# Taking the products of a graph network's last stage straight out of PSUM, with the output stage one pair of tiles later

## The reference: what is computed

```python
# layer 2 (RGCN with basis decomposition, mean aggregation, root weight and bias)
coeff = comp[edge_type]                                   # 8 coefficients for each edge
aggs = [segment_sum(x[src] * coeff[:, b:b + 1], dst) for b in range(8)]
agg = stack(aggs, axis=1) / maximum(deg, 1.0)[:, None, None]
out = concatenate([agg.reshape(N, -1), x], axis=1) @ weight.reshape(-1, 128) + bias
x = layernorm(x + out)                                    # rows without an edge get x @ root + bias only
```

## Time and profile before

| | us |
|---|---|
| median of three runs (1011.98 to 1019.42) | 1016.24 |
| the profiled execution's own time | 1006.45 |
| its span, first to last instruction | 1004.6 |
| GpSimd busy in the span | 702.8 |
| VectorE busy | 816.0 |
| TensorE busy | 827.7 |
| ScalarE busy | 649.2 |
| first gather of the last stage starts at | 698.15 |
| last scatter of the last stage starts at | 992.77 |

### The profile page before, as it was taken

The page is one execution under the profiler, slowest core; times in us unless marked ns, Lnnn a source line. Parts: engine busy times, 40 slices in busy tenths (PEclk is TensorE's granted clock), DMA queues, the critical chain, the costliest instruction groups (busy, mean ns, idle before and its releaser), DMA issues. The chain is left out here.

```text
span 1004.6 us, 19805 instructions
## 1 busy us (share of the span) xinstructions
PE 827.7 (82%) x4972; PEld 663.4 (66%) x4972; DVE 816.0 (81%) x2958; ACT 649.2 (65%) x2960; POOL 702.8 (70%) x702
## 2 busy tenths in 40 slices
PE   4789999999999999999998778774797778687882
PEld 3667777777777777777776666563675667565661
DVE  7999999999999999999997566562696867777793
ACT  3699999999999999999997567663121111121221
POOL 4277777777777777777766466566787878888784
PEclk9999999999999999999999789896799879788996
DMA  6266666666565655656563122212776556565740
GB/s 185 86 199 203 205 195 193 195 194 202 195 205 200 194 193 191 198 197 201 191 188 98 56 72 76 67 58 94 280 269 223 205 201 216 203 215 199 248 171 26
DMA packets 87719, 175.54 MB, mean 175 GB/s; under 512 B 16620, under 2 KB 33032, under 8 KB 81207
## 3 DMA queue, kind: packets, MB, share of 16 engines
q1 hardware_dynamic: 70422, 144.02, 42.2%
q0 software_dynamic: 15744, 29.71, 9.7%
q10 hardware_dynamic: 1440, 0.56, 0.2%
HBM read 105.88 MB, written 70.88 MB: 176 GB/s over the span
## 5 line engine op out<-in xcount | busy, mean ns | idle before, releaser
L648 ACT ACTIVATE junk<-ps 128x128 bf16<-128x128 f32 x884 | 235.7, 300 | 52.4 <-remote 14.2
L605 PE MATMUL ps<-work,w_cen 128*128 128x256 f32 x784 | 199.1, 411 | 14.0 <-DVE work L1029 8.6
L648 ACT ACTIVATION_READ_ACCUMULATOR junk<-ps 128x1 f32 x884 | 199.1, 232 | 0.0
L605 PEld LDWEIGHTS ps<-work,w_cen 128*128 128x128 f32 x784 | 157.7, 207 | 46.8 <-DVE work L1029 15.0
L410 POOL TENSOR_TENSOR work<-work,vec_raw 128x512 f32<-128x512 f32 x98 | 124.2, 1267 | 91.7 <-DVE work L973 90.8
L512 PE MATMUL ps<-w_cen,xT 128*128 128x128 f32 x984 | 163.3, 299 | 0.0
L512 PEld LDWEIGHTS ps<-w_cen,xT 128*128 128x128 f32 x984 | 132.7, 201 | 30.0 <-issue 30.0
L374 POOL DMA_INDIRECT x_table<-agg_all,scat_i x98 | 99.5, 1015 | 71.4 <-issue 27.0
L734 ACT ACTIVATE outb<-agg_now,st 128x128 f32<-128x128 f32 x98 | 34.0, 394 | 169.9 <-DMA out_rows<-outb,scat_i 169.5
L381 POOL DMA_INDIRECT rows<-x_table,src_i x98 | 118.4, 1208 | 31.0 <-issue 29.3
L374 POOL DMA_INDIRECT out_rows<-outb,scat_i x98 | 117.6, 1200 | 30.0 <-issue 28.5
(11 more groups left out here) (139 smaller groups left out, 1481.5 us busy)
## 6 DMA issues: line engine op xcount, KB each, us to landing
coefs<-coef_line SPq DMA_DIRECT2D x49, 1024.0 KB
rows<-in_x SPq DMA_DIRECT2D x97, 256.0 KB
x_table<-work SPq DMA_DIRECT2D x97, 256.0 KB
out_rows<-outb SPq DMA_DIRECT2D x97, 256.0 KB
x_dst_table<-x_dst SPq DMA_DIRECT2D x98, 64.0 KB
rows<-x_dst_table SPq DMA_DIRECT2D x24, 256.0 KB
rows<-in_x,src_i POOLq DMA_INDIRECT x98
same_prev<-mask_line SPq DMA_DIRECT2D x1, 1568.0 KB, 9.0
```

The lines of the kernel that those rows point to most:

```text
L605: last = pe.matmul(MT[b][:, 0:PAIR * D], w_cen[:, W_BASE + m, :], prod[:, b, m, :, :].rearrange("p t d -> p (t d)"), start=(m == 0), stop= ...
L648: last = nc.scalar.activation(junk[:, kind * CH + m, :], bank[:, cols(m, m + 1)], ACT.Square, accum_out=power[:, b, 1, TOP + kind * CH + m ...
```

## The change

In the last stage ScalarE's copy of the transposed rows goes. VectorE's two products read the rows in PSUM, in the bank where TensorE put them. Since a bank is now held until both products are made, `GX` has four banks in place of two: 4, 5, 0 and 1. TensorE waits, before it fills a bank again, for the products of four pairs before, and no longer for ScalarE. The output part of a pair moves one step later on VectorE and ScalarE (`c - 5` for `c - 4`), `OUT_LAG` from 6 to 7, and the loop has one step more. VectorE's order within a step changes: the scan now comes ahead of both products. Apart from that the SP queue issues the coefficient loads of pairs 0 to 2 in steps 120, 121 and 122 of the edge loop, in place of after its last step.

```diff
-OUT_LAG = 6
+OUT_LAG = 7
-    LAST_C = PAIRS + 3
+    LAST_C = PAIRS + 4
-        GT, GX, MT, ST = banks(4, 1), [banks(4, 1), banks(5, 1)], [banks(2, 1), banks(3, 1)], [banks(6, 1), banks(7, 1)]
+        GT, GX, MT, ST = banks(4, 1), [banks(k, 1) for k in (4, 5, 0, 1)], [banks(2, 1), banks(3, 1)], [banks(6, 1), banks(7, 1)]
...
+            def coef_load(q):
+                r = q * PAIR // (TYPE_TILES * LINE_BLOCKS)
+                sp.wait_ge(line_stored[r], 16 * len(blocks_of(r)))
+                need(sp, S["dve_prod"], 2 * (q - COEF_SLOTS + 1))
+                sp.dma_start(coefs[:, q % COEF_SLOTS, :, :, :].rearrange("p t b e -> p (t b e)"),
...
+                if 0 <= c - TYPE_STEP - 10 < COEF_SLOTS:
+                    coef_load(c - TYPE_STEP - 10)
...
-            for q in range(PAIRS):
...
+            for q in range(COEF_SLOTS, PAIRS):
+                coef_load(q)
...
             def step_c(s):                                    # TensorE
-                    need(pe, S["act_g"], s - 1)
+                    need(pe, S["dve_prod"], 2 * (s - len(GX) + 1))
...
             def step_c(s):                                    # ScalarE
-                if c < PAIRS:
-                    act.wait_ge(S["pe_g"], s + 1)
-                    need(act, S["dve_prod"], 2 * (s - 1))
-                    nc.scalar.copy(xT[:, b, 0:PAIR, :].rearrange("p c d -> p (c d)"), GX[b][:, 0:PAIR * D]) \
-                        .then_inc(S["act_g"], 1)
-                if 0 <= c - 4 < PAIRS:
-                    q = c - 4
+                if 0 <= c - 5 < PAIRS:
+                    q = c - 5
...
             def product(h):                                   # VectorE
-                            dve.wait_ge(S["act_g"], s)
+                            dve.wait_ge(S["pe_g"], s)
...
-                            xT[:, 1 - b, 0:PAIR, :].unsqueeze(1).broadcast_to([P, HALF, PAIR, D]), ALU.mult) \
+                            GX[q % len(GX)][:, 0:PAIR * D].rearrange("p (t d) -> p t d", t=PAIR).unsqueeze(1)
+                            .broadcast_to([P, HALF, PAIR, D]), ALU.mult) \
...
                 if last_pair:
-                    dve.wait_ge(S["pe_s"], s - 3)
-                    need(dve, S["act_out"], s - 5)
+                    dve.wait_ge(S["pe_s"], q + 1)
+                    need(dve, S["act_out"], q - 1)
...
-                product(0)
...
+                product(0)
+                if last_pair:
+                    own.need(at)
+                    at = variance(0, PAIR, par)
                 product(1)
```

More of the change, by code:

```diff
@@ L280, in _ @@
             sp.dma_start(w_raw[:, W_POOL, :], pool_w).then_inc(S["pool_in"], 16)
+            def coef_load(q):
[3 more added lines that the diff above has]
+                sp.dma_start(coefs[:, q % COEF_SLOTS, :, :, :].rearrange("p t b e -> p (t b e)"),
+                             coef_line[q * PAIR:(q + 1) * PAIR].rearrange("(o t) b e -> o (t b e)", o=1)
+                             .broadcast_to([P, PAIR * NB * P])).then_inc(coefs_in[q % COEF_SLOTS], 16)
             def step(s):
@@ L589, in _ @@
             pe.wait_ge(S["line_made"], LINES)
+            pe.wait_ge(S["act_a"], GROUPS)
             def step_c(s):
@@ L595, in step_c @@
                     slot = c % GATHER_SLOTS
-                    need(pe, S["act_g"], s - 1)
+                    need(pe, S["dve_prod"], 2 * (s - len(GX) + 1))
                     pe.wait_ge(x1_in[slot], 16 * PAIR * (c // GATHER_SLOTS + 1))
                     for n in range(PAIR):
-                        last = pe.transpose(GX[b][:, cols(n, n + 1)], gathered[:, slot * PAIR + n, :], ident[:, :])
+                        last = pe.transpose(GX[c % len(GX)][:, cols(n, n + 1)], gathered[:, slot * PAIR + n, :], ident[:, :])
                     last.then_inc(S["pe_g"], 1)
@@ L733, in step_c @@
                     for n in range(PAIR):
-                        last = nc.scalar.activation(out_tiles[:, q % SLOTS * PAIR + n, :], y_rows[:, b, n, :],
+                        last = nc.scalar.activation(out_tiles[:, q % SLOTS * PAIR + n, :], y_rows[:, q % 2, n, :],
                                                     ACT.Copy, scale=st[:, 7, n:n + 1])
@@ L1018, in step_c @@
                 b = c % 2
-                last_pair = 0 <= c - 4 < PAIRS
+                last_pair = 0 <= c - 5 < PAIRS
                 def product(h):
@@ L1031, in product @@
                             coefs[:, q % COEF_SLOTS, :, half, :].rearrange("p t m d -> p m t d"),
-                            xT[:, 1 - b, 0:PAIR, :].unsqueeze(1).broadcast_to([P, HALF, PAIR, D]), ALU.mult) \
+                            GX[q % len(GX)][:, 0:PAIR * D].rearrange("p (t d) -> p t d", t=PAIR).unsqueeze(1)
+                            .broadcast_to([P, HALF, PAIR, D]), ALU.mult) \
                            .then_inc(S["dve_prod"], 1)
                 if last_pair:
-                    dve.wait_ge(S["pe_s"], s - 3)
-                    need(dve, S["act_out"], s - 5)
+                    q = c - 5
+                    par = q % 2
+                    dve.wait_ge(S["pe_s"], q + 1)
+                    need(dve, S["act_out"], q - 1)
                     for n in range(PAIR):
-                        t = (s - 4) * PAIR + n
-                        last = dve.scalar_tensor_tensor(y_rows[:, b, n, :], ST[b][:, cols(n, n + 1)],
+                        t = q * PAIR + n
+                        last = dve.scalar_tensor_tensor(y_rows[:, par, n, :], ST[par][:, cols(n, n + 1)],
                                                         inv_deg[:, bass.ds(t, 1)], y_root[:, bass.ds(t * D, D)],
@@ L1043, in step_c @@
                     last.then_inc(S["dve_y"], 1)
-                    dve.wait_ge(S["dve_y"], s - 3)
+                    dve.wait_ge(S["dve_y"], q + 1)
                     for n in range(PAIR):
-                        at = own.mark(dve.bn_stats(bn[:, n, :], y_rows[:, b, n, :]))
-                product(0)
+                        at = own.mark(dve.bn_stats(bn[:, n, :], y_rows[:, par, n, :]))
                 if last_pair:
                     own.need(at)
-                    at = moments(0, PAIR, b)
+                    at = moments(0, PAIR, par)
                 if 0 <= c - 3 < PAIRS:
```

15 lines of the change are left out of this document (4 added, 11 removed).

## The result

Twenty runs of each kernel on one chip: the changed kernel takes 1021.34 us (median; 1014.40 to 1027.17), the kernel before 1016.35 (1008.77 to 1023.86). The ratio is 1.0061, 95% interval 1.0039 to 1.0083: slower, but by less than the 1% that the prediction named as the least it could tell, where 976 us and a ratio of 0.960 were forecast. The profiled execution has a span of 1019.5 us.

A forecast was written before the change was run, and what follows sets the result against it. GpSimd's back-to-back indirect DMAs were taken to bound the last stage: 42.1 us freed, 2.3 given back at the end, so 40 less; about 966.5 profiled plus the carried 9.8 gave 976 us, range 964 to 996.

The forecast's parts named there:

- Step 1: GpSimd, last stage: unhindered transfers take 253.5 us against 295.6, saving 42.1; a four-DMA step takes 5.18 instead of 6.0.
- Step 4: VectorE's order, last stage: scan ahead of both products keeps 4.48 us a pair, up to 4.6, below GpSimd's 5.18.
- VectorE steps over 5.2, with GpSimd waiting in mid-stage: Sign, last stage: steps over 5.2 us, GpSimd waiting for ScalarE's output, would show product price or VectorE order wrong.
- Step 8: End of last stage: waits for outputs give back 2.3 us; last scatter ends at 954 instead of 993.75, 40 less.
- Steps 2, 3 and 7: Dropping ScalarE's copy saves nothing; PSUM product stays 1.21 us; early coefficient loads in edge loop cost 0, at worst 3.7.
- The first gather later than 698: Sign, start of last stage: a first gather after 698 us would show the early coefficient loads' zero cost wrong.
- Steps 5 and 6: Last stage: TensorE needs 4.38 us a pair, below 5.18; output a pair later costs nothing, slack 3.8 us, then growing.
- VectorE and TensorE become the bound: Rival, last stage: TensorE at half clock in some steps leaves less saving, 986 to 1003 us; chance 0.12.
- the product still holds GpSimd: Rival, last stage: four DMAs stay at 6.0 us, nothing is freed, 1008 to 1020 us; chance 0.07.

The follow-up runs named there:

- e1: Changed kernel with VectorE's order put back, the first product again ahead of the moments and the scan: 1006.25 us, ratio 1.0018 to the kernel before.
- e4: Kernel before with VectorE's order alone changed, the scan ahead of both products, rows still copied by ScalarE: 1001.59 us, ratio 0.9962.
- "again" runs: One further chip, before at 1014.17 us: changed kernel 1018.01, before repeated 1011.07, changed with one memset behind each transfer 1018.08, before with PSUM products alone 1020.22.

## Why the prediction was wrong

**Step 1 was right in what it freed**: GpSimd is busy 42.8 us less, where its means of 0.98 and 1.01 give 41.0 (the 42.1 holds the waits too). So `tensor_tensor` with both inputs in SBUF did lengthen the transfers, against the inference in the Trainium skill, "SBUF — State Buffer", "Who interferes with whom". What was wrong is the sentence that followed, that a step of four takes 5.18: a pair takes 5.08 with the memsets on the chip without late signals, and 5.87 to 5.93 in three profiles of the changed kernel on chips with them, 4 x 1.47 to 1.48.

**Step 4 failed.** "TensorE can begin that one two VectorE steps earlier" is true, and TensorE did; but the step then took the 3.62 us of the product as all that the scan waits for. The end of a product is not its signal: at the first scan they lay 10.1 us apart, and from 740 to 950 us VectorE's scan stood 44.4 us for TensorE. The order itself is innocent (e1, e4). My line "VectorE steps over 5.2, with GpSimd waiting in mid-stage" is what the profile shows.

**Step 8 failed with it**, since it has GpSimd finish a pair every 5.18 us and VectorE every 4.48. Since GpSimd is no longer the last to finish a pair, the gathers run to the end of their lead, seven pairs, and the end is the pipeline's length: 60.8 us behind the last gather for 41.9. So of the 42.8 us, from the first gather to the last 12.1 are saved (253.7 to 241.6), the end gives back 18.9, and the last stage is 6.8 us longer; 8.3 more are the later first gather, within the scatter of the edge steps. The four ratios of the changed kernel, 1.004 to 1.006, hold less than this one profile's sum.

**Steps 2, 3 and 7 held**: no copy missed, 1.21 us a product, and early loads at 0.9994. "The first gather later than 698" was a poor sign, as it moves by 20 us from profile to profile, with early loads or without. **Steps 5 and 6** took full clock and a thin slack. The product after the first stall, from 735.45 on, took 6.43 us where the one before took 3.62; but the granted clock from 790 to 955 us was 0.88 for 0.89 before, so the clock hardly differs between the two kernels. In the kernel with the memsets on the chip without late signals the clock was 0.99 from 700 to 870 us, and scatters waited 6.6 us in all for output.

The rival "VectorE and TensorE become the bound" (0.12) named the engines but not the mechanism, and its price, a quarter or half of the steps at half clock, isn't what was paid. The rival "the product still holds GpSimd" (0.07, 1008 to 1020) lies next to the measured time by chance: the transfers at 969 and 1002 ns refute its mechanism. On the chip without late signals the forecast's own sum came out in the kernel with the memsets: last stage 258.3 us for 255.8, ratio 0.955 for 0.960. I had a warning and didn't weigh it: the trace of before has late signals in its edge steps. Its last stage has transfers 1.51 us apart on average, just slower than the 1.46 at which held signals were worked off later. That a second limit lay 2 to 3% below the one that I removed fits both paces, but it is argued and not shown: it doesn't explain why not one of 124 signals was late there.

**Open:** what in the chip holds the signals up, what starts the holding, and why one chip of the five named here doesn't; whether the first comparison's chip, which has late signals too, is one of these. Not shown either: the changed kernel itself on the chip without late signals. No version tried that computes the whole output beats the kernel before by 1% on a chip with late signals; each needs four transfers a pair.

## What to carry over

When a bound is removed, ask at which rate the next one sits, and look for waits whose producer had long been done: here, on four chips of five, the count of transfers per pair and not their duration on the engine set the pace. A gain measured on one chip can be absent on another; repeat the kernel before in every comparison, and look at a part of the program that the edit doesn't touch before crediting the edit. A tiny filler instruction behind a DMA issue is no pause: it hides in the 0.3 us that the engine stands anyway, and ten of them overlap to 0.39 us. Measure the pause before reading its effect.

## What the runs showed of the hardware

- On four chips, and in the first comparison, recorded semaphore increments of TensorE came up to 15 us (26 in the kernel with five transfers) behind the recorded end of the matmul, while GpSimd issued indirect transfers close together; a stream of n of them that held signals was clear some 1.42 to 1.47 n us after its start, by the means of twelve profiles. Recorded increments of the other engines were within 0.04 us, one excepted. Held signals then come together, 0.04 us apart (738.20 and 738.24 us in the changed kernel).
- In the edge steps, where transfers stand more alone, 73 of 140 late signals came 1.4 to 1.6 us after the last transfer's start (kernel before, profiled beside the "again" runs).
- On one chip none of this happened, and the kernel before took 968.6 us there instead of 1004.7 to 1016.4.
- `tensor_tensor` of 128x1024 with one input in PSUM leaves GpSimd's indirect transfers at 0.97 and 1.00 us; with both in SBUF they averaged 1.21 and 1.20, and 1.08 and 1.26 with VectorE's other order.
- Ten GpSimd memsets of 128x1, 0.13 us each, started 0.03 us apart and took 0.39 us together.
